# Self-attention of a decoder layer: the spread reciprocals of the row sums go through TensorE as two float16 parts instead of one float32

## The reference, cut to what matters

```
xn = layernorm(x); q, k, v = split(xn @ w_qkv)          # 16 heads of 32
scores = where(causal, (q / sqrt(32)) @ k.T, -1e10)
attn = softmax(scores, axis=-1)                         # exp(s - max) / row sum
x = x + (attn @ v) @ w_out
```

## Time and profile before

| | |
|---|---|
| three executions | 798.13, 796.03, 798.06 us; median 798.06 |
| the profiled execution | 796.43 us, its span 794.7 us |
| PE busy | 685.9 us (86%), PEld 610.3 (77%) |
| DVE, ACT, POOL busy | 503.6 (63%), 308.7 (39%), 312.5 (39%) |
| self-attention | from 0 to about 336 us of the span |

### The profile page before, as it was taken

How to read it: one execution, slowest core, us unless ns; L and a number is a source line. 1 busy time by engine, 2 the same in 40 slices (tenths; PEclk the granted TensorE clock), 3 DMA queues, 4 the chain that set the end, 5 groups by cost and what they waited for, 6 DMA issues and landing times. The chain is left out here.

```text
span 794.7 us, 19084 instructions
## 1 busy us (share of the span) xinstructions
PE 685.9 (86%) x6040; PEld 610.3 (77%) x6041; DVE 503.6 (63%) x1456; ACT 308.7 (39%) x984; POOL 312.5 (39%) x534
## 2 busy tenths in 40 slices
PE   4569999999999996578999999999999986239995
PEld 4569898888889895477988888888889975228884
DVE  4577887878778867186645464656565557626663
ACT  3356566666656564143232232323232343102220
POOL 0556756666675756144000101010101046435662
PEclk9789999999999998679999999999999998559998
DMA  9265876656656466196212222222222046246530
GB/s 340 77 107 91 124 138 142 140 111 139 142 116 143 104 131 150 50 319 232 97 64 80 80 79 79 79 79 79 79 79 79 0 132 185 80 136 183 185 118 17
DMA packets 142885, 95.07 MB, mean 120 GB/s; under 512 B 110846, under 2 KB 115070, under 8 KB 142720
## 3 DMA queue, kind: packets, MB, share of 16 engines
q1 hardware_dynamic: 137184, 82.00, 40.0%
q0 software_dynamic: 5664, 12.61, 5.2%
HBM read 56.14 MB, written 18.77 MB: 94 GB/s over the span
## 5 line engine op out<-in xcount | busy, mean ns | idle before, releaser
L400 ACT ACTIVATE prob<-prob,shift 128x128 f32<-128x128 f32 (+1 forms) x256 | 114.6, 449 | 117.1 <-POOL shift L328 116.6
L60 PE MATMUL b_bank<-w_hi 128*128 128x256 f32 (+1 forms) x576 | 119.8, 331 | 7.3 <-DVE w_lo L1191 7.2
L1003 ACT CAST w_hi<-b_bank 128x256 fp32r<-128x256 f32 (+1 forms) x144 | 60.3, 446 | 160.6 <-PE b_bank L60 143.4
L60 PE MATMUL b_bank<-w_lo,w_hi 128*128 128x256 f32 (+1 forms) x576 | 115.2, 323 | 0.0
L60 PE MATMUL b_bank<-w_hi,w_lo 128*128 128x256 f32 (+1 forms) x576 | 114.7, 322 | 0.0
L60 PEld LDWEIGHTS b_bank<-w_hi 128*128 128x128 f32 x576 | 89.8, 195 | 16.0 <-DVE w_lo L1191 8.1
L600 DVE CUSTOM_DVE_ANT_0 prob<-a_s,mask 128x128 f32<-128x128 f32 (+1 forms) x256 | 79.6, 348 | 32.7 <-PE a_s L476 32.6
L1191 DVE TENSOR_TENSOR w_lo<-b_bank,w_hi 128x256 fp32r<-128x256 f32 (+1 forms) x144 | 68.3, 507 | 47.2 <-ACT w_hi L1003 47.1
L60 PEld LDWEIGHTS b_bank<-w_lo,w_hi 128*128 128x128 f32 x576 | 91.3, 195 | 8.1
L60 PEld LDWEIGHTS b_bank<-w_hi,w_lo 128*128 128x128 f32 x576 | 90.7, 194 | 7.6
L328 POOL TENSOR_SCALAR shift<-nmax 128x2 f32<-128x2 f32 x128 | 42.4, 332 | 105.7 <-DVE nmax L600 102.1
(11 more groups left out here) (169 smaller groups left out, 1372.1 us busy)
## 6 DMA issues: line engine op xcount, KB each, us to landing
stage<-in_w SPq DMA_DIRECT2D x8, 1024.0 KB, 5.5
xin<-in_x SPq DMA_DIRECT2D x8, 512.0 KB, 4.1
xr<-in_x SPq DMA_DIRECT2D x8, 512.0 KB, 4.1
x<-xr SPq DMA_DIRECT2D x8, 512.0 KB, 3.2
xin<-x SPq DMA_DIRECT2D x8, 512.0 KB, 4.3
b_cin_t<-in_ctx_t SPq DMA_DIRECT2D x8, 512.0 KB, 3.6
b_cin<-in_ctx SPq DMA_DIRECT2D x8, 512.0 KB, 3.5
xr<-x SPq DMA_DIRECT2D x8, 512.0 KB, 4.3
```

Source lines behind the costliest of these rows:

```text
L60: ins = pe_matmul(out, a, b, start=first and i == 0, stop=last and i == len(steps) - 1)
L400: a = nc.scalar.activation(prob[:, e % NPROB, cols], prob[:, e % NPROB, cols], ACT.Exp, scale=-1.0, bias=shift[:, e, q:q + 1], accum_out=r ...
L1003: nc.scalar.copy(hi, src).then_inc(job_hi, 1)
```

## The change

The reciprocals are multiplied by 2**23 and split on DVE into a float16 high part and a float16 rest (`rinv_part`, two more small instructions behind the reciprocal, and two more waits). POOL's repeating copy takes both parts, 512 float16 numbers in each partition instead of 256 float32, and waits for the second DVE instruction instead of the reciprocal. PE does four float16 matmuls of 128 columns instead of two float32 ones and sums up high and low part in PSUM, against a float16 identity that POOL makes once at the start. DVE's product multiplies by 2**-23 as well. Nothing else differs.

```diff
--- before.py
+++ after.py
@@ -95,7 +95,10 @@
         p_part = sb("p_part", [P, NPROB, 2, 3 * P], F16)
         pt = sb("pt", [P, NPT, 2 * 3, P], F16)
         rsum, rinv = sb("rsum", [P, G, TB, HG]), sb("rinv", [P, G, TB, HG])
-        rinv_wide = [sb(f"rinv_wide{i}", [P, TB, HG, HD]) for i in range(2)]
+
+        rinv_part = sb("rinv_part", [P, 2, TB, HG], F16)
+        rinv_wide = [sb(f"rinv_wide{i}", [P, 2 * TB, HG, HD], F16) for i in range(2)]
+        ident_half = sb("ident_half", [P, P], F16)
         o_sb = [sb(f"a_o_sb{i}", [P, S]) for i in range(2)]
         ot_hi, ot_lo = sb("ot_hi", [P, G, S], F32R), sb("ot_lo", [P, G, S], F32R)
         raw = sb("a_raw", [P, 4, DC, D])
@@ -115,8 +118,8 @@
         p_hi_done, p_done = sem("p_hi_done"), sem("p_done")
         pt_in = [sem(f"pt_in{j}") for j in range(HG)]
         v_mid_done, v_done = sem("v_mid_done"), sem("v_done")
-        rinv_done, wide_done, av_done, r_done, rs_done = (sem(n) for n in (
-            "rinv_done", "wide_done", "av_done", "r_done", "rs_done"))
+        rinv_done, wide_done, av_done, r_done, rs_done, rinv_hi_done, rinv_lo_done = (sem(n) for n in (
+            "rinv_done", "wide_done", "av_done", "r_done", "rs_done", "rinv_hi_done", "rinv_lo_done"))
         on_done, ot_hi_done, ot_done = sem("on_done"), sem("ot_hi_done"), sem("ot_done")
 
         SLOTS = {0: ["q2"], 1: ["k2"], 2: ["q3"], 3: ["k3"], 4: ["u0"], 5: ["u1"], 6: ["w0"], 7: ["w1"], 8: ["X0", "X1"],
@@ -296,6 +299,8 @@
 
             nc.gpsimd.affine_select(out=mask[:, P:], in_=mask[:, P:], compare_op=ALU.is_ge, fill=NEG, base=0,
                                     pattern=[[-1, P]], channel_multiplier=1).then_inc(consts, 1)
+            pool.wait_ge(consts, 5)
+            nc.gpsimd.tensor_copy(ident_half[:], ident[:]).then_inc(consts, 1)
 
             def next_rstd(k):
 
@@ -338,9 +343,10 @@
                     before = groups_before(h, WIDE_LAG, n)
                     wait(pool, r_done, before - 1)
                     pool.sem_inc(tick_pool, 1)
-                    pool.wait_ge(rinv_done, before + 1)
+                    pool.wait_ge(rinv_lo_done, before + 1)
                     pool.sem_inc(tick_pool, 1)
-                    nc.gpsimd.tensor_copy(rinv_wide[g % 2][:], free_ap(rinv[:, g, :, :], 0, [[HG, TB], [1, HG], [0, HD]]))\
+                    nc.gpsimd.tensor_copy(rinv_wide[g % 2][:], free_ap(rinv_part[:, 0, :, :], 0,
+                                                                       [[HG, 2 * TB], [1, HG], [0, HD]]))\
                         .then_inc(wide_done, 1)
                 g = group_at(h, OT_LAG, n)
                 if g is not None:
@@ -367,7 +373,7 @@
                 for h in range(H):
                     slot(n, h)
 
-        CONSTS = 5
+        CONSTS = 6
 
         @block.scalar
         def _(act):
@@ -503,9 +509,10 @@
                 m.then_inc(av_done, 1)
                 pe.wait_ge(wide_done, before + 1)
                 for q in range(TB):
-                    m = nc.tensor.matmul(o_ps[:, 1, q * P:(q + 1) * P],
-                                         rinv_wide[g % 2][:, q, :, :].rearrange("p j d -> p (j d)"), ident[:],
-                                         start=True, stop=True)
+                    for z in range(2):
+                        m = nc.tensor.matmul(o_ps[:, 1, q * P:(q + 1) * P],
+                                             rinv_wide[g % 2][:, z * TB + q, :, :].rearrange("p j d -> p (j d)"),
+                                             ident_half[:], start=z == 0, stop=z == 1)
                 m.then_inc(r_done, 1)
 
             pe.wait_ge(consts, CONSTS)
@@ -615,12 +622,21 @@
                 g = group_at(h, ON_LAG, n)
                 if g is not None:
                     dve.wait_ge(rs_done, groups_before(h, ON_LAG, n) + 1)
-                    nc.vector.tensor_tensor(o_sb[g % 2][:], o_ps[:, 0, :], o_sb[g % 2][:], ALU.mult).then_inc(on_done, 1)
+                    nc.vector.scalar_tensor_tensor(o_sb[g % 2][:], o_ps[:, 0, :], 2.0 ** -23, o_sb[g % 2][:], ALU.mult,
+                                                   ALU.mult).then_inc(on_done, 1)
                 g = group_at(h, RINV_LAG, n)
                 if g is not None:
                     before = groups_before(h, RINV_LAG, n)
                     dve.wait_ge(ex_done, before * HG + HG)
                     nc.vector.reciprocal(rinv[:, g, :, :], rsum[:, g, :, :]).then_inc(rinv_done, 1)
+                    wait(dve, wide_done, before)
+                    dve.wait_ge(rinv_done, before + 1)
+                    dve.sem_inc(tick, 1)
+                    nc.vector.tensor_scalar(rinv_part[:, 0, :, :], rinv[:, g, :, :], 2.0 ** 23, None, ALU.mult)\
+                        .then_inc(rinv_hi_done, 1)
+                    dve.wait_ge(rinv_hi_done, before + 1)
+                    nc.vector.scalar_tensor_tensor(rinv_part[:, 1, :, :], rinv[:, g, :, :], 2.0 ** 23,
+                                                   rinv_part[:, 0, :, :], ALU.mult, ALU.subtract).then_inc(rinv_lo_done, 1)
                 if head_at(h, 0, n) is not None and (not isinstance(n, int) or n < B - 1):
                     if h in (1, 2):
                         norm_stats(n + 1, h - 1)
```

## The result

| | before | after |
|---|---|---|
| median of four executions each, same chip | 797.12 us | 811.23 us (810.62 to 812.3) |
| the profiled execution, its span | 796.43, 794.7 us | 810.62, 808.8 us |
| PE, DVE, ACT, POOL busy | 685.9, 503.6, 308.7, 312.5 us | 681.5, 528.2, 307.5, 318.7 us |

The kernel is slower by 14.1 us, ratio 1.018 (95% interval 1.0155 to 1.0205). The forecast was 802.5, its range ended at 809: the direction was right, the size was not. PE does 4.4 us less work and DVE 24.6 us more.

A forecast was written before the change was run, and what follows sets the result against it. PE looked like the bound, but its waits for DVE and POOL decided: +0.58 us a batch six times (3.5), first batch 1.2, last 0.5, behind it 0.1, together +5.3 us, given as 802.5 us, range 796.5 to 809.

The forecast's parts named there:

- DVE's term: Two small dependent DVE instructions behind the reciprocal add 0.50 us before its successor; ends 0.22 and 0.85.
- Leg 1: PE's scores of group 0 to scores of group 1: DVE's +0.50 against 0.37 of room gives +0.13 us.
- DVE has 0.37 us to give there: Between scores of groups 0 and 1, DVE can run 0.37 us later before PE must wait.
- Leg 2: Scores of group 1 to values of group 0: DVE's 0.50 plus POOL's longer copy 0.21 gives +0.71 us.
- Everything added comes out in this leg in full: From group 1's scores to group 0's values, additions to DVE in slot 5 or POOL in slot 6 count fully.
- Leg 3: Values of group 0 to scores of group 3: spreading block 0.23 us shorter, but y0 needs ot_hi, so -0.13 us.
- Leg 4: Group 3's scores to next group 0's: block saves 0.23 us, but k1 needs k0's low part, so -0.13 us.
- The first and last batch: First batch +1.2 us from DVE and copy in full; last batch +0.5, and +0.1 behind it.
- The lock: Rival: the new DVE pair stands still until POOL's L349 ends, adding 0.85 us; +13.2, 811.3 us, chance 0.12.
- The matmuls don't get shorter: Rival: float16 weights load no faster than float32's in PE's spreading block; +7.4, 805.5 us, chance 0.07.
- no difference: Rival: the DVE pair costs 0.30 us and POOL's copy nothing; about -0.3, 797.8 us, chance 0.20.
- PE is the bound everywhere: Rival: PE's 0.23 us saved in each of 32 spreading blocks all counts; 7.4 us go, 790.7 us, chance 0.08.

The follow-up runs named there:

- the moved kernels: Changed kernel and kernel before, each with reciprocal and POOL's copy two slots later (the former with its DVE pair): 794.2 us (0.9979) and 793.18 us (0.9967).
- the placement: Kernel before plus an unused tensor of 32 bytes a partition where the changed kernel allocates rinv_part: 798.16 us, ratio 1.0025.
- the pair alone: Kernel before plus the two new DVE instructions and their waits, results unused, float32 matmuls and short copy kept: 808.85 us, ratio 1.0154.
- a kernel of -1.6%: Changed kernel with reciprocal and pair two slots later, copy on ACT, ot_hi ahead of exp, rinv_part allocated last: 783.91 us (0.9843); counterpart without the change 786.28 (0.9878).
- the kernel with the copy on ACT: Changed kernel with reciprocal and pair two slots later and the repeating copy on ACT instead of POOL: 795.6 us, ratio 1.0005.

## Why the prediction failed, point by point

**The failed step is DVE's term, "I take 0.50 for what is added between reciprocal and successor".** It measured 0.61, 0.70, 0.96 and 1.08 us in slots 9, 5, 1 and 13. It had two faults. The plain cost is 0.61 (slot 9): the multiplication starts 0.33 behind the reciprocal, 0.14 of it waiting for its result, and the two aggregates of the earlier trace rows showed only 0.22 a step. And the hold was priced for slot 5 alone, and as a rival at 0.12. It was looked for at the second instruction, because that has two SBUF inputs; in the steady batches the first is the one held, with one. (The second is held in the same way when it is the one that starts under POOL's: 317.04 here, and slot 7 of the moved kernels.) Its place could have been worked out from before: L349 ran from 177.49 to 178.22 in slot 1 (reciprocal at 177.56) and from 169.47 to 170.20 in slot 13 (reciprocal at 169.28). If the multiplication ends 0.03 behind it and the successor comes 0.20 later, the additions are 0.78, 0.77 and 1.04 for slots 1, 5 and 13, where 0.96, 0.70 and 1.08 were measured. The 0.03 and the 0.20 are known only from the changed kernel, and slot 1's excess is the idle time ahead of L552. The L558 that was only stretched by 0.15 was taken as evidence against a hold; it said nothing of an instruction of another form.

The Trainium skill, "SBUF — State Buffer", section "Who interferes with whom", names two kinds of DVE instruction that share ports with GpSimd: those with two SBUF inputs, and copies, casts and `tensor_scalar` in their two-port modes, of which it says that a GpSimd instruction that came first blocks them in full. The prediction used the first kind only. The trace agrees with the second: the 21 ends 0.02 to 0.04 us behind POOL's. Which mode the instruction ran in no profile here shows. For larger instructions the blocking is not in full here: L615 starts 0.03 us behind POOL's L317 (164.85) and ends only 0.41 after it, although it takes 0.55 alone.

**Leg 1, forecast +0.13, measured +0.74.** "DVE has 0.37 us to give there" was right (the scores follow the maxima by 0.15 now and followed by 0.49): 0.96 in slot 1 and 0.07 more on the way, less 0.34, is 0.69 (9.54 against the 8.85 of the prediction's batch).

**Leg 2, forecast +0.71, measured +0.15.** Both terms came, 0.70 on DVE and 0.21 on POOL. But slot 5's tensor_scalar (L565) is now behind L355 and takes 0.55 instead of 0.82, and the last lower part of v (L317) takes 0.67 instead of 1.08, since it now starts 0.03 ahead of the low part of p on DVE, which is the one that is held (1.05 instead of 0.56); before, with starts 0.01 apart, POOL's was. That gave back 0.27 and 0.41; with 0.08 less on the rest of the way it is 0.15. That the order of the last two turned this way was luck: their starts differ by hundredths of a microsecond, and it turned in batch 4 of the kernel before as well. POOL's rows of slots 6 and 7:

```profile
161.43 0.80 POOL L348 COPY rinv_wide<-rinv_part 128x512 f16<-128x512 f16 x1
...
164.82 0.67 POOL L317 TENSOR_TENSOR v_part<-v_rest,v_part 128x256 bf16<-128x256 f32 x1
165.57 0.40 POOL L333 TENSOR_SCALAR shift<-nmax 128x2 f32<-128x2 f32 x1
```

"Everything added comes out in this leg in full" failed because each duration in the chain depended on what ran beside it.

**Leg 3, forecast -0.13, measured +0.27.** The block went from 0.47 to 0.20, as forecast (0.24). But `ot_hi` ends 0.22 later behind the values than before, as the exp ahead of it waits for the shift above, 0.40 instead of 0.21, and y0 follows it by 0.13, not by 0.05: +0.17 instead of -0.13. The rest, 0.10, is the pace of y0 and y1, of which the placement explains 0.07.

**Leg 4, forecast -0.13, measured +0.71.** "k1 needs DVE's low part of k0" was right. That low part ends at 180.53, 7.33 behind group 3's scores, against 6.09 before: 1.08 of the pair in slot 13, 0.27 of the low part of p ahead of it (0.82 instead of 0.55 us, beside POOL's later parts of v), less 0.11 behind it. Less the room of 0.58 that k1 had, this is 0.66. So not all of it is the pair's: with the pair alone leg 4 grows by 0.52.

**The first and last batch**, forecast +1.2 and +0.6, measured +1.8 and +1.3. The first is the same mis-sized term. The last is not only that: PE waits 2.17 us for POOL's L317 ahead of the values (0.84 before), and behind it the granted clock is 0.50, its lower level, from 316 to 318, where it was 1.00 before; y0's first four matmuls take 2.05 us instead of 1.21.

```profile
316.00:317.00 1.00, 1.00 (x13) 0.85 (x6) 0.86 (x3) 0.93 (x5) 0.87 (x3) 0.50 0.74 145
```

**The rivals.** "The lock" had the sum, 811.3, and the mechanism: a DVE instruction that stands until POOL's ends. Its legs were +0.48, +1.06, -0.13, +0.27, against +0.74, +0.15, +0.27, +0.71, so the total agrees partly by chance: legs 1 and 4 were too low by 0.7 together and leg 3 by 0.40, leg 2 too high by 0.91. It named the second instruction as the one that waits, which is so only outside the steady batches. "The matmuls don't get shorter" is out (0.20 a block), "no difference" too. "PE is the bound everywhere" is out for this kernel; with the preparation off the chains its share of 0.7 us in two legs appears.

## What to carry to other kernels

Before small instructions are put on DVE, ask what POOL does at that moment in every slot where they stand, not only in one, and ask again after each move: eight numbers cost 0.17 or up to 0.67 us here, and the pair met another POOL instruction in its new place. Where two instructions meet within hundredths of a microsecond, a duration from the profile holds for that order only, and a shift of either side may give or take 0.4 us. Work that shortens a busy engine by splitting its operand pays where nothing waits behind the splitting: here the same change was +1.8% in one place and stood in a kernel of -1.6% in another, of which -1.2% came without it.

## What was not expected of the hardware

- A `tensor_scalar` of 8 float32 numbers to float16, with one SBUF input, was held until POOL's `tensor_tensor` of 256 columns ended (0.24 to 0.62 us instead of 0.17, 21 of 21). A `scalar_tensor_tensor` of 8 numbers with two SBUF inputs was held in the same way (0.64 to 0.67 us). Under POOL's `tensor_tensor` L308, which raises 2 columns to a power and takes 0.72 us, the first took its 0.17 (149.31 in the kernel with the copy on ACT).
- In the other direction, POOL's `tensor_tensor` took 1.08 instead of 0.67 where DVE's with two SBUF inputs began within 0.01 us of it, and 0.68 where DVE's came 0.34 later, which then took 0.76 instead of 0.55. With starts 0.01 apart either of the two may be the stretched one (batches 3 and 4 of the kernel before).
- 32 bytes more in each partition ahead of the tensors moved the pace of float32 matmuls of 512 columns from 0.229 to 0.233 us.
- Float16 matmuls of 128 columns with their own loads came every 0.06 us within a block, float32 ones every 0.11.
- The granted clock fell from 1.00 to 0.50 behind waits of 0.80 and 0.94 us in batch 1 of the moved kernel, and stayed at 1.00 where the same waits came in batch 2.
